# Per-head attention: the value products of two cells issued next to one another

## The reference

```python
xn = _layernorm(x, ln_gamma, ln_beta)
q = proj(Wq) / math.sqrt(DH); k = proj(Wk); v = proj(Wv)      # each [B, 16, T, 16]
scores = jnp.einsum('bhid,bhjd->bhij', q, k)
scores = scores + rel[:, jnp.clip(i[:, None] - i[None, :], 0, 128)][None]
scores = jnp.where(i[:, None] >= i[None, :], scores, -jnp.inf)
attn = jax.nn.softmax(scores, axis=-1)
y = jnp.einsum('bhij,bhjd->bhid', attn, v)
return x0 + y.transpose(0, 2, 1, 3).reshape(B, T, D) @ Wo.T
```

## Time and profile before

| | before |
|---|---|
| median of three runs | 2776.13 us |
| the profiled execution | 2777.85 us, span 2776.0 us |
| busy: PE, DVE, ACT, POOL | 2217.6, 1620.4, 969.2, 453.9 us |
| stretch of the heads' cells, 1843 to 2583 us: PE, DVE, ACT | 685.7, 512.4, 418.5 us of 742 |
| granted TensorE clock: whole span, that stretch | 0.863, 0.98 |
| value products (L2097) | 1536 records, 162.4 us busy |

### The profile page before, as it was taken

The page is one execution under the profiler, slowest core; times in us unless marked ns, Lnnn a source line. Parts: engine busy times, 40 slices in busy tenths (PEclk is TensorE's granted clock), DMA queues, the critical chain, the costliest instruction groups (busy, mean ns, idle before and its releaser), DMA issues.

```text
span 2776.0 us, 39998 instructions
## 1 busy us (share of the span) xinstructions
PE 2217.6 (80%) x13342; PEld 1613.4 (58%) x13342; DVE 1620.4 (58%) x4577; ACT 969.2 (35%) x1964; POOL 453.9 (16%) x402
## 2 busy tenths in 40 slices
PE   4489999908999857999994276378999999999476
PEld 2478888806888736888883144324444454444254
DVE  6744443353555675433444897266866766875695
ACT  4122233203333331232331331325555556556321
POOL 4320000040000134000003553411011011000242
PEclk8799999958999878999997555669999999999755
DMA  7110101020000122001002100242322323230001
GB/s 237 41 59 26 28 28 32 22 76 1 1 1 1 35 83 73 28 28 32 28 28 60 49 12 0 61 65 59 48 42 53 48 47 63 37 43 2 5 22 39
DMA packets 83735, 114.14 MB, mean 41 GB/s; under 512 B 12162, under 2 KB 74020, under 8 KB 80420
## 3 DMA queue, kind: packets, MB, share of 16 engines
q1 hardware_dynamic: 77396, 94.53, 15.5%
q0 software_dynamic: 6144, 17.05, 1.9%
HBM read 68.90 MB, written 42.64 MB: 40 GB/s over the span
## 4 chain that ended last, share of the span: by engine, by line
PE 63%; DVE 21%; ACT 5%; issue 5%; DMA 3%; POOL 2%; another core or an unknown queue 1%; SPq 0%; ACTq 0%; DVEq 0%; POOLq 0%
PE psum L774 9%; PE psum L776 9%; PE psum L775 9%; PE psum L122 5%; PE psum L2097 4%; PE psum L123 4%; PE psum L124 4%; PE psum L2076 4%; PE psum L2056 3%; PE psum L861 3%; PE psum L2080 3%; DVE junk L1961 2%; PE psum L1426 2%; DVE m L1949 1%; DVE stats L155 1%
## 5 line engine op out<-in xcount | busy, mean ns | idle before, releaser
L1898 ACT ACTIVATE pt<-psum 128x512 f32<-128x512 f32 (+3 forms) x768 | 338.9, 491 | 283.2 <-DVE psum L1987 196.2
L739 DVE SCALAR_TENSOR_TENSOR h<-psum,xg,sg 128x128 f32<-128x128 f32 x592 | 166.9, 345 | 415.2 <-PE psum L861 415.2
L774 PE MATMUL psum<-w_hi,xt_hi 128*128 (+1 forms) x720 | 286.3, 398 | 33.7 <-DVE xt_lo L704 33.7
L548 ACT ACTIVATE sg<-psum 128x512 f32<-128x512 f32 x180 | 107.6, 598 | 584.0 <-PE psum L776 543.0
L775 PE MATMUL psum<-w_lo,xt_hi 128*128 (+1 forms) x720 | 284.5, 395 | 0.0
L776 PE MATMUL psum<-w_hi,xt_lo 128*128 (+1 forms) x720 | 284.5, 395 | 0.0
L2056 PE MATMUL psum<-ks,qs 96*128 96x512 bf16 (+3 forms) x768 | 232.9, 342 | 49.7 <-DMA ks<-qk_scr 19.9
L2076 PE MATMUL psum<-qs,ks 99*128 99x512 bf16 (+3 forms) x768 | 236.8, 332 | 18.4 <-ACT pt L1898 11.4
L774 PE MATMUL psum<-w_hi,ht_hi 128*128 (+1 forms) x720 | 220.5, 306 | 8.3 <-DVE x L754 8.0
L1961 DVE CUSTOM_DVE_ANT_0 junk<-psum,band_q 128x256 bf16<-128x256 f32 (+1 forms) x512 | 204.8, 400 | 22.3 <-PE psum L2056 12.0
L776 PE MATMUL psum<-w_hi,ht_lo 128*128 (+1 forms) x720 | 205.9, 286 | 0.0
(11 more groups left out here) (281 smaller groups left out, 4884.4 us busy)
## 6 DMA issues: line engine op xcount, KB each, us to landing
xg<-w_dram SPq DMA_DIRECT2D x54, 256.0 KB, 3.3
qk_scr<-parts SPq DMA_DIRECT2D x32, 384.0 KB, 2.5
qs<-qk_scr SPq DMA_DIRECT2D x96, 128.0 KB, 7.0
ks<-qk_scr SPq DMA_DIRECT2D x96, 128.0 KB, 7.7
xg<-rows_in SPq DMA_DIRECT2D x74, 132.0 KB, 2.2
rows_out<-yb SPq DMA_DIRECT2D x74, 128.0 KB, 1.7
x<-x_dram SPq DMA_DIRECT2D x4, 1024.0 KB, 9.3
out_dram<-x SPq DMA_DIRECT2D x4, 1024.0 KB, 4.4
```

The lines of the kernel that those rows point to most:

```text
L739: ins = dve.scalar_tensor_tensor(out=h[i % 2][:, e, :], in0=u[:, e, :], scalar=xg[j % XSLOT][:, at:at + 1], in1=sg[i % 2][:, e, :], op0=AL ...
L774: pe.matmul(out, a[0], b[0], start=first, stop=False)
L1898: act.activation(pt[n % NPT][:, 0:q1 - q0], st_bank(n)[:, 0:q1 - q0], ACT.Exp).then_inc(*exped.up())
```

## The change

The values of two cells are put into the order together. `due` now holds single steps. When it holds three, two of them are taken out at once; it keeps one, and is at three again two cells later. So after the scores of every even cell k come the values of cells k - 2 and k - 1, and after odd cells none. After cell 0 of the next unit come those of cells 10 and 11. The other lines of the diff only adapt to the new form of the list.

```diff
-                    due.append([("value", (u, cell))])
+                    due.append(("value", (u, cell)))
                     if len(due) > 2:
-                        yield due.pop(0)
+                        yield [due.pop(0), due.pop(0)]
...
                     if tokens[0][0] == "value":
-                        placed.add(tokens[0])
+                        placed.update(tokens)
                         continue
...
-            for tokens in due:
-                order.extend(tokens)
-                placed.add(tokens[0])
+            order.extend(due)
+            placed.update(due)
             return order + sum(tail, [])
```

## The result

The changed kernel takes 2791.93 us (median of six runs), the kernel before, on the same chips, 2775.37: a ratio of 1.0063 (95% interval 1.0051 to 1.0075). It is slower by some 17 us, where 12.8 less were forecast.

What follows compares the result with a forecast made beforehand. PE was taken as the bound, DVE next. Eight plain units x 1.1 = 8.8, six x 0.5 = 3.0, two x 0.5 = 1.0: 12.8 us less, 2763.3 us; own range 2757 to 2770, given range 2752 to 2782.

Steps and rivals of the forecast that it cites:

- part 1: Value steps on PE: 190 separate runs become 96, so 94 switches of 0.21 us go, 19.7 us less PE time.
- a gap between banks: Where paired cells write different banks, the gap stays (13 of 19.7 us); within the no-gain rival, 2774 us, chance 0.21.
- open weight loads: Second cell's first loads, 0.12 us, stand open in each of 94 pairs: 11 us, time 2774; chance 0.03.
- part 2: Waits that moved value steps, second-half copy and transposes bring with them: nothing new is waited for, cost nothing.
- part 3: Longer value bursts, in which PE feeds neither DVE nor ACT: cells 7 to 2 -0.8 us, cells 3 to 6 -0.3.
- 0.2 us a pair: Sign of being wrong: PE's waits at fourth heads of even cells grow by over 0.2 us a pair.
- rival (c): Cells with maxima: DVE becomes the bound, idle at each double burst; +19 us, 2795 us, chance 0.16.
- the backlog B: DVE's work still queued when a value burst starts, read as 1.06 and 1.25 us at two value steps.
- 29.0 less all four: DVE's limit for cells 7 to 2, 29.0 - 4B: 24.0 us with B = 1.25, 24.8 with 1.06.
- Cells 3 to 6: Little DVE work: two switches less, -0.42 us, and one added wait of 0.1 to 0.2 give -0.3 us.
- part 4: Six units with projections gain 0.5 us each, half a plain unit's; units 14 and 15, without maxima, 0.5 each.
- 0.93: DVE backlog in us at which 29.0 - 4B equals today's 25.26 us for cells 7 to 2.

Runs made afterwards that it cites:

- DVE and ACT were out of the way: Changed kernel without VectorE's bias, its maxima reductions cut to two columns a piece, and ScalarE's exponentials cut to 128 columns: 2678.61 us, 0.9743 of the kernel before.
- the run with the lighter maxima: Changed kernel, but VectorE's reductions for the maxima look at two columns of each piece: 2697.29 us, 0.9797 of the kernel before.
- the better order: Changed kernel, but values of cells 0 and 1 separate, and the head with VectorE's bias last in cells 0, 2, 8 and 10: 2738.92 us, 0.9948 of before.
- VectorE nearly idle: Changed kernel without VectorE's bias and with its maxima reductions cut to two columns a piece: 2715.35 us, 0.9778 of the kernel before.

## Why the prediction was wrong, point by point

**The switches (part 1) were right.** There are 96 runs, no gap between banks, and 94 times 0.21 us less; where DVE and ACT were out of the way, a stretch gave 0.22 to 0.24. That the trace of before has a run of 24 records without gaps was a sound basis, and the rivals of a gap between banks or of open weight loads are refuted by the run of 1.91 us for two 512-wide cells: there is no room in it for 0.12 us of open loads.

**"All of this I cost at nothing" (part 2) failed in one item.** I went through what the moved step waits for, and not through what waits behind it: the values of cell 1 were the cover of a wait of the transpose of the maxima. Its price is 0.56 us in each unit with that step, shown by the run with cells 0 and 1 apart; its cause by the run with the lighter maxima. The earlier tail was in that list as well. In a plain unit of the better order it costs 0.26 us, and at the batch ends with projections it gives.

**The bursts (part 3) failed, with the sign.** For cells 7 to 2 I took 24.5 us; they take 5.57 + 7.08 + 5.95 + 8.00 = 26.6, against 25.26 before. The step that failed is "I take 24.5, a little above PE's, since both limits are near". I bounded the stretch by DVE's time and by PE's with the waits of today, each by itself, and took the larger. The runs showed two things in its place.

The first is that PE and DVE are tied to each other through ACT. In cell 10, where no burst stands ahead after the change, the bias queues behind a full ring of maxima, ACT starts late, and PE stops for 0.62 us at the fourth head. That is over the 0.2 us a pair which the prediction itself named as the sign of being wrong. The runs without the bias and with the head last show it: the stretch 9, 10 is then 6.34 and 6.33 us, shorter than with the same cut or head in the order of before (6.43 and 6.80). The mechanism stands in the prediction, under rival (c), as an argument without a price; its place is even named (even cells, fourth head). A price was in reach: bias 1.26 instead of 0.43 us behind the score, which is about the backlog in the earlier trace rows.

The second is that the backlog B was read at two value steps, 1.06 us at cell 0 and 1.25 at cell 4, and taken for all; only the one of cell 4 becomes one of the four double bursts. At the value step of cell 10 the trace of before has 0.30, and DVE idles for 1.27 us there. A longer burst finds this unchanged: 0.41 and 1.38 with the pairs, 0.53 and 1.26 with the pairs and no bias. At the burst of cell 8 (2394.69), just behind the stop in cell 10, DVE had been dry for 0.12 us; it gets one more maximum and works until 0.87 us behind the burst's start. With the four backlogs as they were (1.26, 1.34, 0.87 and 0.42) the prediction's own sum, 29.0 less all four, gives 25.1 us and not 24.0 to 24.8. DVE's work was estimated 0.6 us low besides (23.0 us busy in these cells, not 22.4), and three pauses of 0.14 us between its own instructions, there in both kernels, were left out; that makes 26.1 of the 26.6.

At the other two the forecast was right: at 2387.61 DVE works until 2388.95 (1.34 us) and idles for 0.61, and behind the burst of cell 4 it idles for 0.69, forecast 0.5 to 0.8.

**Cells 3 to 6.** I forecast -0.3; they take 12.67 us instead of 12.54, +0.13, with the lost cover of 0.56 in it.

**Batch ends (part 4).** I forecast 0.5 us of gain in each of the six units with projections. Units 0 and 1 together are 3.4 us longer, 5 and 9 1.2 each; 4 and 8 with the unit before each are longer by only 0.1 and 0.2, since the earlier tail helps there. Units 11 and 12 are 5.2 longer, of which 2.9 is twice the plain unit's. Units 14 and 15, without maxima, give 0.7 and 0.5 us, as forecast (0.5 each).

**The account of a plain unit.** Forecast -1.1, measured +1.47. Switches: -1.26. Cover of cell 4: +0.56. Bias: the difference between the orders falls from 1.47 to 0.63 without it, so 0.84. VectorE's load in all, bias and cover included: without the maxima's reductions the difference is -0.5 instead of 1.47, so some 2.0. That leaves about 0.6, found only as a remainder, which I put down to a starved DVE and a full ring; no run shows it by itself. The rest of 0.7 to 0.8 stays with VectorE nearly idle: 0.4 of it is ScalarE's, in the stretches 7, 8 and 5, 6, and 0.4 stands in the stretch 1, 2. For that one the wait on the ring is shown; that it is all of it was not tried.

**The rival that came true** is (c), at 2795 us and 0.16. Its time was close, in part by luck. Its reason, that B falls below 0.93 with the double bursts, doesn't hold: the four backlogs are 0.97 in the mean, and the 0.42 among them was 0.30 before the change already. What held is the argument behind it, of the late bias, ACT and the fourth head; it accounts for 0.84 us of a plain unit's 2.7 of new waits.

## What to carry to other kernels

A step that occupies one engine for a microsecond is, for the others, the time in which they catch up: before moving it, ask at both of its places whose queue is full without it, and go through what stands right behind it, not only what it waits for. Two engines that are each below their limit can still be tied into one chain by a third; bounds taken engine by engine are then too low. Read a queue's backlog at every place that a bound uses, and not at two of them. And the short operation in the middle (here a bias of 0.3 us) should go where its queue is empty, just behind a burst, or just ahead of one; which of the two is better was not the same in each cell, so the place is measured cell by cell. Merge only where the stretch table says that it pays.

## What the runs showed of the hardware

A change between the 17-column value products and full-width matmuls costs 0.21 us beyond streaming (0.10 ahead of a run and 0.13 behind, less the ordinary 0.02), and between two groups of 17-column ones nothing, also when the second group writes another PSUM bank and accumulates there: two cells of 512 queries take 1.91 us, 1.71 of it streaming. The pattern of a plain unit repeats from unit to unit mostly to 0.02 us a stretch, with single stretches 0.1 to 0.4 us longer (5, 6 in unit 6 of the changed kernel: 6.62 instead of 6.26). The sum of stretches taken from different kernels gave a third kernel's unit (37.15 us, measured 37.14 in unit 10).
